# Reordering the first stage of a fused latent-attention and factorised-FFN kernel, with head 1's weights made in unit 0

## The chip, the cores and the metric

One core of a Trainium2 chip runs the kernel; it is launched as one program. The metric is the device time of one execution in microseconds.

## The reference, cut to what matters

```python
xn = layernorm(x)                       # x: 2048 x 512, float32
q = (xn @ wq) per head -> q_nope (128), q_pe (64)     # 16 heads
kva = xn @ wkv_a -> ckv (128), k_pe (64)
ckv = ckv * rsqrt(mean(ckv * ckv) + 1e-6) * kv_norm_scale
k_nope, v = (ckv @ wkv_b) per head
q_pe, k_pe = rope(q_pe), rope(k_pe)
scores = (q_nope @ k_nope.T + q_pe @ k_pe.T) / sqrt(192), causal
attn = softmax(scores) @ v, heads joined, @ wo
ffn = sum over 8 factors of xn @ factors[r], / sqrt(8) + bias
out = x + attn + ffn
```

## The kernel before, in words

The keys are never expanded per head. All heads share 128 normalised latents and 64 turned key elements of each of the 2048 positions; each head's key weights are folded into its query weights (w_abs), its value weights into the output weights (w_vo). Numbers that need float32 precision are kept as pairs of float16 tensors, a high and a low half, and a product is three matmuls (`three`, lines 390 to 392): high by high, high by low, low by high.

**The first stage** (t = 0 to 19, written out by hand on every engine) goes over 16 tiles of 128 rows, two of them a pair p2. SP loads a pair of x (line 1394). VectorE takes mean and variance (`norm_stats`, lines 894 and 898), ScalarE the root (`norm_scale`, 649), VectorE its reciprocal and the shift (904, 906), and ScalarE normalises tile by tile into `xn` (`normalize`, 643), two buffers that overlay `rot`. TensorE transposes (462); ScalarE writes the high half (692), VectorE the low one (1062). `latent_product` on TensorE makes latents and rope keys of a tile. `latent` on ScalarE sums squares (660, 663), `latent` on VectorE takes the reciprocal and turns the keys' first parts (1074 to 1080), `latent_scale` on ScalarE (674) and `turned_keys` on GpSimd (1286) finish them in `kt`, four buffers. `value_parts` on ScalarE copies them to `vH` (681), and that on GpSimd makes `vL` (1278). `keys` transposes them on TensorE (483, 484), with high halves from ScalarE (687, 688) and low ones from VectorE (1087, 1089). Between these stand the weights of heads 0 and 1: the sum over the partitions of squares (`norm`), `scale_pair` on VectorE (921 to 940), transposes of wq and wkv (`wq_transpose`, `kv_transpose`; 1003 to 1028 on VectorE), `w_abs` (1037, 1039) and `w_pe` (732 on ScalarE, 1044 on VectorE). The latent weights `wa` are scaled first by their own norm (`scale_latent`, 835, 1225). At the end stand q_rope(0), q_latent(0) and q_latent(1) on TensorE, the rope parts of the query on ScalarE and GpSimd (763, 1332) and squares of the weights of heads 2 and 3 on ScalarE (695).

**The units** are 64: head by head, for chunks 3, 2, 1, 0 of 512 query rows. A unit has four row blocks r of 128 rows; a row block has chunk + 1 pieces of up to 512 keys (chunk 3, row block 0: 512, 512, 384, 256). `scores` writes one of four banks, `maxima` and `row_max` on VectorE find the maximum of the row over all pieces (1123, 1125, 1135, 1142), `exps` on ScalarE frees the bank (774; it is the first exponential, so the program has a table load ahead of it), `high_parts` (784) and `low_parts` on GpSimd (1341) split the result, and SP issues DMA transposes of it into `pT` (1513). The next unit multiplies them with the values. There are four `ex` buffers, so an exponential waits for the low part four pieces back.

**What sets the order.** Every engine goes through its instructions in the order written; semaphores join them. `fills(i, r)` lists the extra work of unit i behind row block r (weights of later heads, queries of the next unit, outputs), and each engine takes its part of that list in its order. Matmul banks are handed out by `bank_order`. SP's queue is in the order written too: loads of x and of weights (`load_wq` waits for `p_tq` at h - 1 and for the squares of two heads before, `load_wp` for `v_wpe`), then `store_chunk` of the transposed x, then

```python
for m in range(2, 4):
    load_wq(m)
load_wp(2)
store_abs(0)
store_abs(1)
store_pe(0)
```

and then each unit's DMAs. On ScalarE, `squares` (695) waits for the load of its weights: "sqp" for `d_wp`, 64 for each load of a pair of heads.

Of the kernel before, what the change touches and what calls it, by code (L numbers as in the profile page):

```python
# [36 lines left out]

FFN = tuple(QT * c + t for c in ORDER for t in range(QT))
# [10 lines left out]
def chunk(i):  # L49

    return ORDER[i // H]

# [43 lines left out]
def fills(i, r):  # L96

    out = []
    if r == 0:
        if 1 <= i < NU - 1:  # L100
            out.append(("q", i + 1))
        if 1 <= i <= H:
            out.append(("nv", i - 1))
        if i == SQUARED + 1:
            out.append(("nf", 0))
        if i and i % 2 == 0 and i + 2 < H:
            out.append(("nrm", i + 2))
# [11 lines left out]
    if r == 1:  # L119
        if i == 0:  # L120
            out.append(("nrm", 2))
        if i % 2 == 0 and i + 2 < H:
            out.append(("wpe", i + 2))
        if i % 2 == 0 and i + 2 < H:
            out.append(("tq", i + 2))
        if i + 2 <= H + 2:
            out.append(("tkv", i + 2))
# [8 lines left out]
    if r == 2 and i % 2 == 0 and i + 2 < H:  # L136
        out.append(("wpe_low", i + 2))
# [5 lines left out]
    if r == 2:  # L143
        if 1 <= i <= H:
            out.append(("wvo", i - 1))
        if i + 2 < H:
            out.append(("wabs", i + 2))
# [31 lines left out]
def bank_order():  # L179

    pre = []
    for t in range(NT + 4):
        if t < NT:
            pre.append(("xt", t))
        if t == 0:
            pre.append(("na", 0))
        if t == 7:
            pre.append(("nrm", 0))
        if t in (8, 11):
            pre += [("tq", t // 3 - 2), ("tkv", t // 3 - 2)]  # L190
        if t in (10, 13):
            pre.append(("wabs", t // 3 - 3))
        if t % 2 == 1 and 0 <= t // 2 - 2 < NP:
            pre.append(("kT", t // 2 - 2))
        if t == NT + 1:
            pre.append(("pe", 0))
        if t == NT + 2:
            pre.append(("q", 0))
        if t == NT + 3:
            pre.append(("q", 1))  # L200
# [4 lines left out]
def build(nc, x, wq, wkv_a, wkv_b, wo, kvs, factors, bias, rope_t, rope_n, out):  # L205
    ctx = ExitStack()
    with ctx:
# [77 lines left out]
        with nc.sbuf_tensor("early", [P, 2, 4, 2, KE, CH], F16) as region:  # L285
# [8 lines left out]
        xn = rot  # L294
# [11 lines left out]
            "a_sqv", "a_sqo", "a_r4", "a_r8", "a_sqa", "a_sqp", "a_sq0", "a_sq1", "a_sqk", "a_sqf", "a_wa", "a_sd", "a_xn", "a_xt", "a_sq", "a_rms", "a_kk", "a_vH", "a_kT", "a_ff", "a_wpe", "a_wo",  # L306
# [9 lines left out]
            "g_zero", "g_const", "g_sk", "g_sv", "g_fac", "g_bias", "g_rot", "g_parts", "g_pL", "g_kk", "g_vL",  # L316

            "d_wq0", "d_wq1", "d_wo", "d_wp", "d_wk0", "d_wk1", "d_wk2", "d_wk3", "d_wv0", "d_wv1", "d_scl", "d_tab", "d_x0", "d_x1", "d_w", "d_wa", "d_bias",
# [47 lines left out]
        def s_bank(n):  # L366
            return ps[:, n % SBANKS, :]
# [20 lines left out]
        def _(e):  # L388
# [76 lines left out]
            def latent_product(t):  # L465
# [6 lines left out]
                for k4 in range(KE):  # L472
                    ins = three(latent_bank(t // 2)[:, t % 2, :], [x_tile(t, a)[:, k4, :] for a in range(2)],
# [47 lines left out]
            def scores(i, r, p):  # L521
# [83 lines left out]
            for t in range(NT + 4):  # L605
                p = t // 2
                if t < NT:
                    transpose_x(t)
                if t == 0:
                    norm(("na", 0), ("a_sqa",), nra[:, :])  # L610
# [11 lines left out]
                if t == NT + 1:  # L622
                    q_rope(0)
                if t == NT + 2:
                    q_latent(0)
                if t == NT + 3:
                    q_latent(1)
            for i in range(NU + 2):
                for r in range(QT):
                    if i < NU:  # L630
                        for p in range(chunk(i) + 1):
# [6 lines left out]
        def _(e):  # L638
            def normalize(t):
# [3 lines left out]
                e.activation(xn[:, t % 2, :], x_in(t), ACT.Identity, bias=rstd[:, 2, t:t + 1],  # L643
# [34 lines left out]
            def value_parts(p2):  # L678
                ts = slice(2 * p2, 2 * p2 + 2)
                e.wait_ge(z["a_kk"], p2 + 1)  # L680
                e.activation(vH[:, ts, :], kt[p2 % 4][:, :, 0:LORA], ACT.Copy).then_inc(z["a_vH"], 1)

            def keys(p2):
                b = bank(("kT", p2))
                cols = slice(2 * p2 * P, (2 * p2 + 2) * P)
# [4 lines left out]
            def transpose_x(t):  # L690
                e.wait_ge(z["p_xt"], t + 1)
                e.activation(x_tile(t, 0), by4(bank(("xt", t))), ACT.Copy).then_inc(z["a_xt"], 1)
# [130 lines left out]
            normalize(0)  # L823
            norm_scale(1)
            e.wait_ge(z["d_wa"], 16)
            square_sum(wa_f.rearrange("p k n -> p (k n)"), 0, nra[:, :]).then_inc(z["a_sqa"], 1)
            for t in range(NT + 4):
# [3 lines left out]
                if t < NT:  # L831
                    transpose_x(t)
                if t == 0:
                    e.wait_ge(z["v_lat"], 1)
                    e.activation(wa[:, 0, :, :], wa_f, ACT.Identity, bias=eps[:, 2:3], scale=lat[:, 0:1]).then_inc(
                        z["a_wa"], 1)
                if t % 2 == 0 and 0 <= p - 2 < NP:
                    latent_scale(p - 2)
                    value_parts(p - 2)
# [20 lines left out]
            for kind in ("sqk", "sqp", "sq0", "sq1"):  # L860
                squares(kind, 2)
            for i in range(NU + 2):
                for r in range(QT):
# [3 lines left out]
                    for kind, n in fills(i, r):  # L867
                        if soon and kind == "pv":
                            fill(kind, n)
                    for p in range(last + 1):  # L870
# [4 lines left out]
                        if p == 2 and r < 2:  # L875
# [754 lines left out]
```

## Time and profile before

| what | us |
|---|---|
| median of 3 runs | 1525.97 (1525.07 to 1528.10) |
| the profiled execution, its own time | 1529.43 |
| its span | 1527.5 |
| TensorE busy | 1479.1 (97%) |
| VectorE busy | 1012.5 (66%) |
| ScalarE busy | 974.4 (64%) |
| GpSimd busy | 904.7 (59%) |
| mean granted TensorE clock | 0.994 |

The span is that of the profiled execution on its core; 1.9 us lie outside it. Times in the rows below count from its start. PE is TensorE, PEld its weight load, DVE VectorE, ACT ScalarE, POOL GpSimd, and SPq SyncE's queue of DMA issues. "[1.99 <-ACT ex L774]" behind a row says how long the engine was idle before it, and what it waited for.

### The profile page before, as it was taken

The numbers are of one execution on the slowest core, as the hardware profiler recorded it, in microseconds if no ns is written. First come the engines' busy times: TensorE is split into PE (matmuls) and PEld (weight loads), VectorE is DVE, ScalarE is ACT, GpSimd is POOL, SyncE is SP. The second block draws the span as 40 slices with busy tenths as digits, with TensorE's granted clock in tenths as the row PEclk, the third lists the DMA queues.
The fourth block names the chain that finished last, engine by engine and source line by source line (L and its number), as shares of the span: only waits on it lengthen the run. The fifth ranks groups of instructions, "written<-read, shape, count | busy, mean of one in ns | idle before, by whom it ended". The sixth has DMA issues, their size and how long they took to land.

```text
span 1527.5 us, 25754 instructions
## 1 busy us (share of the span) xinstructions
PE 1479.1 (97%) x7908; PEld 758.3 (50%) x7908; DVE 1012.5 (66%) x2563; ACT 974.4 (64%) x2418; POOL 904.7 (59%) x905
## 2 busy tenths in 40 slices
PE   5789999999999999999999999999999999999997
PEld 4444455555544544444445454545545555455553
DVE  6666777767777766655455565656656666676786
ACT  6777676777767476666466667665646666654553
POOL 1367777775655455666465656566645655664552
PEclk9999999999999999999999999999999999999998
DMA  6369989998776588787677677886856677854654
GB/s 219 105 124 206 205 181 189 187 189 163 150 154 139 114 174 168 142 175 138 131 143 139 134 139 146 153 162 134 155 117 138 136 140 149 157 133 98 120 119 99
DMA packets 646598, 227.83 MB, mean 149 GB/s; under 512 B 599360, under 2 KB 612160, under 8 KB 646080
## 3 DMA queue, kind: packets, MB, share of 16 engines
q1 hardware_dynamic: 646464, 226.20, 73.0%
q8 instruction: 65, 1.06, 0.3%
q14 instruction: 69, 0.57, 0.1%
HBM read 65.67 MB, written 17.83 MB: 55 GB/s over the span
## 4 chain that ended last, share of the span: by engine, by line
PE 80%; ACT 7%; DVE 6%; issue 3%; POOL 3%; DMA 1%; SPq 0%; POOLq 0%; ACTq 0%; DVEq 0%
PE ps L390 16%; PE ps L391 16%; PE ps L392 16%; PE ps L534 6%; PE ps L539 6%; PE ps L540 6%; PE ps L536 6%; PE ps L535 6%; ACT ex L774 3%; POOL st L1341 1%; DVE gm L1123 1%; DVE ps L1125 1%; POOL q L1332 1%; DMA st<-x_in 0%; ACT sqr L695 0%
## 5 line engine op out<-in xcount | busy, mean ns | idle before, releaser
L1341 POOL TENSOR_TENSOR st<-ex,st 128x512 f16<-128x512 f32 (+3 forms) x640 | 637.7, 1015 | 504.3 <-ACT st L784 494.5
L774 ACT ACTIVATE ex<-ps,nm,scales 128x512 f32<-128x512 f32 (+3 forms) x640 | 452.5, 709 | 466.8 <-DVE nm L1142 452.8
L1123 DVE TENSOR_REDUCE gm<-ps 128x1 f32<-128x512 f32 (+1 forms) x384 | 249.0, 669 | 176.8 <-PE ps L540 172.6
L784 ACT ACTIVATE st<-ex 128x512 f16<-128x512 f32 (+3 forms) x640 | 341.4, 561 | 5.9
L534 PE MATMUL ps<-kTh,q 128*128 128x512 f16 (+3 forms) x640 | 223.2, 349 | 8.5 <-ACT ex L774 8.4
L539 PE MATMUL ps<-kRh,q 128*128 128x512 f16 (+3 forms) x640 | 222.9, 348 | 4.5 <-POOL q L1332 4.5
L390 PE MATMUL ps<-pT,vH 128*128 128x512 f16 (+3 forms) x640 | 222.4, 347 | 2.4 <-DMA pT<-st 2.4
L536 PE MATMUL ps<-kTh,q 128*128 128x512 f16 (+3 forms) x640 | 223.0, 348 | 0.0
L535 PE MATMUL ps<-kTl,q 128*128 128x512 f16 (+3 forms) x640 | 223.0, 348 | 0.0
L540 PE MATMUL ps<-kRl,q 128*128 128x512 f16 (+3 forms) x640 | 223.0, 348 | 0.0
L391 PE MATMUL ps<-pT,vH 128*128 128x512 f16 (+3 forms) x640 | 222.5, 348 | 0.0
L392 PE MATMUL ps<-pT,vL 128*128 128x512 f16 (+3 forms) x640 | 219.3, 348 | 0.0
L1176 DVE SCALAR_TENSOR_TENSOR acc<-ps,rden,acc 128x512 f32<-128x512 f32 x256 | 189.7, 743 | 4.1 <-PE ps L392 3.7
L1332 POOL TENSOR_TENSOR q<-rot,q 32x512 f16<-32x512 f32 x128 | 149.0, 1164 | 28.6 <-ACT q L763 16.5
L1125 DVE CUSTOM_DVE_ANT_0 ps<-ps,cmask 128x256 f32<-128x256 f32 (+3 forms) x256 | 133.0, 519 | 26.1 <-PE ps L540 23.4
L774 ACT ACTIVATION_READ_ACCUMULATOR ex<-ps,nm,scales 128x1 f32 x640 | 125.7, 196 | 0.0
L1100 DVE SCALAR_TENSOR_TENSOR q<-ps,q 128x512 f16<-128x512 f32 x64 | 44.2, 691 | 114.6 <-ACT q L757 114.6
L390 PE MATMUL ps<-wV,oT 128*128 128x512 f16 x256 | 97.7, 382 | 4.7 <-issue 3.1
L534 PEld LDWEIGHTS ps<-kTh,q 128*128 128x128 f16 x640 | 62.7, 98 | 77.9 <-ACT ex L774 16.8
L391 PE MATMUL ps<-wV,oT 128*128 128x512 f16 x256 | 97.7, 382 | 0.0
L392 PE MATMUL ps<-wV,oT 128*128 128x512 f16 x256 | 97.7, 382 | 0.0
L390 PE MATMUL ps<-xT,wA 128*128 128x512 f16 x256 | 97.0, 379 | 0.0
(200 smaller groups left out, 2145.2 us busy)
## 6 DMA issues: line engine op xcount, KB each, us to landing
wA<-w_abs SPq DMA_DIRECT2D x48, 256.0 KB, 3.0
wV<-w_vo SPq DMA_DIRECT2D x48, 256.0 KB, 3.0
pT<-st SPq DMA_TRANSPOSE x640, 3.3
fland<-factors_in SPq DMA_DIRECT2D x28, 256.0 KB, 3.3
wP<-w_pe SPq DMA_DIRECT2D x24, 256.0 KB, 3.0
wsq<-wq_in SPq DMA_DIRECT2D x16, 256.0 KB, 3.9
wso<-wo_in SPq DMA_DIRECT2D x16, 256.0 KB, 3.1
w_abs<-wA SPq DMA_DIRECT2D x16, 256.0 KB, 2.3
```

The costliest lines, as they stand in the source:

```text
L390: e.matmul(o, a[0], b[0], start=first, stop=False)
L391: e.matmul(o, a[0], b[1], start=False, stop=False)
L392: return e.matmul(o, a[1], b[0], start=False, stop=last)
L534: e.matmul(b, q[:, i % 2, 0, qs], kTh[:, ks], start=True, stop=False)
L535: e.matmul(b, q[:, i % 2, 0, qs], kTl[:, ks], start=False, stop=False)
L536: e.matmul(b, q[:, i % 2, 1, qs], kTh[:, ks], start=False, stop=False)
L539: e.matmul(b, q[:, i % 2, 2, qs], kRh[:, ks], start=False, stop=False)
L540: e.matmul(b, q[:, i % 2, 2, qs], kRl[:, ks], start=False, stop=True).then_inc(z["p_s"], 1)
L774: e.activation(ex[:, n % NEX, 0:keys], s_bank(n)[:, 0:keys], ACT.Exp, bias=nm[:, (i * QT + r) % 4:(i * QT + r) % 4 + 1], scale=scales[:, p ...
L784: e.activation(stage(n, keys)[:, :, 0, :], ex[:, n % NEX, 0:keys].rearrange("p (t n) -> p t n", n=P), ACT.Copy).then_inc(z["a_pH"], 1)
L1123: e.tensor_reduce(m, b, AX_X, ALU.max).then_inc(z["v_max"], 1)
L1341: e.tensor_tensor(s[:, :, 1, :], ex[:, n % NEX, 0:keys].rearrange("p (t n) -> p t n", n=P), s[:, :, 0, :], ALU.subtract).then_inc(z["g_pL" ...
```

## The change

The pairs of tiles are taken in another order: chunk 3's (whose queries come first) and then chunks 0, 1, 2. `PAIRS` maps the pair's place in the order to the pair. The first pair of x is loaded in two DMAs. ScalarE squares the latent weights ahead of the first normalize, and VectorE makes `wa` ahead of the second round. `xn` overlays `ex`. On VectorE, norm_stats goes behind keys in odd t, and norm_scale into even t; on ScalarE latent stands ahead of keys. q_rope(0) and q_latent(0) go to t = 13. `vH` is written by GpSimd. The weights and queries of head 1 are made in unit 0, as fills, as are the squares of head 3's query weights. The first two pieces of unit 0 are scored ahead of the last keys.

```diff
+PAIRS = tuple(QT * c // 2 + n for c in (ORDER[0],) + tuple(range(NC - 1)) for n in range(QT // 2))
...
 def fills(i, r):
     out = []
+    if i == 0:
+        out += [[("tq", 1), ("tkv", 1), ("sq1", 2)], [("wabs", 1), ("nrm", 2), ("wpe", 2)],
+                [("q", 1), ("tq", 2), ("tkv", 2), ("wpe_low", 2)], [("wabs", 2)]][r]
...
-        xn = rot
+        xn = ex
...
         def s_bank(n):
-            return ps[:, n % SBANKS, :]
+            return ps[:, (n + 2) % SBANKS, :]
...
@@ scores @@
-                elif n == 0:
+                if n == 2:
                     e.wait_ge(z["v_kva"], NP)
                     e.wait_ge(z["a_kk"], NP)
-                    e.wait_ge(z["v_kT"], NP)
+                if i == 0 and r == 0 and p < NC - 1:
+                    e.wait_ge(z["v_kT"], (p + 2) * QT // 2)
...
@@ the first stage on TensorE @@
+                if t == 0:
+                    norm(("na", 0), ("a_sqa",), nra[:, :])
                 if t < NT:
                     transpose_x(t)
...
-                if t in (8, 11):
-                    wq_transpose(t // 3 - 2)
-                    kv_transpose(t // 3 - 2)
-                if t in (10, 13):
-                    w_abs(t // 3 - 3)
+                if t == 9:
+                    wq_transpose(0)
+                    kv_transpose(0)
+                if t == 11:
+                    w_abs(0)
...
-                if t == NT + 1:
+                if t == 13:
                     q_rope(0)
+                    q_latent(0)
                 if t == NT + 2:
-                    q_latent(0)
-                if t == NT + 3:
-                    q_latent(1)
+                    scores(0, 0, 0)
+                    scores(0, 0, 1)
...
@@ the first stage on ScalarE @@
             norm_scale(0)
-            normalize(0)
-            norm_scale(1)
             e.wait_ge(z["d_wa"], 16)
             square_sum(wa_f.rearrange("p k n -> p (k n)"), 0, nra[:, :]).then_inc(z["a_sqa"], 1)
+            normalize(0)
...
                 if t % 2 == 0 and 0 <= p - 2 < NP:
                     latent_scale(p - 2)
-                    value_parts(p - 2)
+                if t % 2 == 0 and p + 1 < NP:
+                    norm_scale(p + 1)
...
-                if t == 12:
+                if t == 10:
                     w_pe(0)
-                if t == NT + 3:
+                if t == 14:
                     q_latent(0)
+                if t % 2 == 1 and 0 <= p - 1 < NP:
+                    latent(p - 1)
+                if t == NT:
+                    rope_parts(0)
                 if t % 2 == 1 and 0 <= p - 2 < NP:
                     keys(p - 2)
-                if t % 2 == 1 and 0 <= p - 1 < NP:
-                    latent(p - 1)
-                if t % 2 == 1 and p + 2 < NP:
-                    norm_scale(p + 2)
-            q_latent(1)
-            rope_parts(0)
-            for kind in ("sqk", "sqp", "sq0", "sq1"):
+            for kind in ("sqk", "sqp", "sq0"):
                 squares(kind, 2)
...
@@ the first stage on VectorE @@
             norm_stats(0)
             norm_scale(0)
+            scale_latent()
             norm_stats(1)
-            norm_scale(1)
+            e.wait_ge(z["a_wa"], 1)
+            e.scalar_tensor_tensor(out=wa[:, 1, :, :], in0=wa_f, scalar=lat[:, 0:1], in1=wa[:, 0, :, :],
+                                   op0=ALU.mult, op1=ALU.subtract).then_inc(z["v_wa"], 1)
...
-                if t == 7:
+                if t == 8:
                     scale_pair(0)
-                if t in (8, 11):
-                    wq_transpose(t // 3 - 2)
-                    kv_transpose(t // 3 - 2)
-                if t in (10, 13):
-                    w_abs(t // 3 - 3)
-                if t == 13:
+                if t == 10:
+                    wq_transpose(0)
+                    kv_transpose(0)
+                if t == 12:
+                    w_abs(0)
                     w_pe(0)
-                if t == NT + 2:
+                if t == 14:
                     q_rope(0)
-                if t == NT + 3:
                     q_latent(0)
+                if t == NT + 1:
+                    latent(NP - 1)
+                if t % 2 == 0 and p + 1 < NP:
+                    norm_scale(p + 1)
                 if t % 2 == 1 and 0 <= p - 2 < NP:
                     keys(p - 2)
-                if p + 2 < NP:
-                    if t % 2 == 0:
-                        norm_stats(p + 2)
-                    else:
-                        norm_scale(p + 2)
-            q_latent(1)
+                if t % 2 == 1 and p + 2 < NP:
+                    norm_stats(p + 2)
...
@@ units on VectorE @@
+                    if (i, r) == (0, 3):
+                        q_latent(1)
...
@@ GpSimd @@
-                e.wait_ge(z["a_vH"], p2 + 1)
+                e.wait_ge(z["a_kk"], p2 + 1)
+                e.tensor_copy(vH[:, ts, :], values).then_inc(z["g_vH"], 1)
...
             for p2 in range(NP):
                 turned_keys(p2)
-                value_parts(p2)
-            q_rope(0)
-            rope_parts(0)
+                if p2 == NP - 2:
+                    rope_parts(0)
+                if p2 < NP - 2:
+                    value_parts(p2)
...
@@ SP @@
-                e.wait_ge(z["v_xt"], QT * (c + 1))
+                e.wait_ge(z["v_xt"], QT * (c + 2))
...
                 load_wq(m)
             load_wp(2)
             store_abs(0)
-            store_abs(1)
             store_pe(0)
...
+                    if (i, r) == (0, 2):
+                        store_abs(1)
```

## Rows read from the trace of the kernel before

**Rows 1.** Busy time and matmul clock by stretch: us, PE, PEld, DVE, ACT, POOL, PEclk, DMA
```profile
0.00:96.00 96.00, 63.22 (x441) 44.90 (x441) 60.98 (x191) 66.74 (x179) 27.72 (x51) 0.95 0.46 140
82.80:86.20 3.40, 3.40 (x10) 1.27 (x9) 1.39 (x2) 2.74 (x8) 1.75 (x2) 0.51 0.00 0
96.00:1527.50 1431.50, 1415.91 (x7467) 713.43 (x7467) 951.51 (x2373) 907.69 (x2241) 876.97 (x855) 1.00 0.75 150
```

**Rows 2.** Timeline of ScalarE, first stage: start, us, engine, line, operation, tiles
```profile
...
9.39 0.83 ACT L695 ACTIVATE sqr<-vH 128x768 bf16<-128x768 f32 x1
...
25.29 0.80 ACT L643 ACTIVATE rot<-st,rstd 128x512 f32<-128x512 f32 x1
...
26.47 0.62 ACT L695 ACTIVATE sqr<-wsq 128x512 bf16<-128x512 f32 x1
...
27.70 0.36 ACT L687 ACTIVATE kTh<-ps 128x256 f16<-128x256 f32 x1
...
29.23 0.28 ACT L649 ACTIVATE rstd<-mv,eps 128x2 f32<-128x2 f32 x1
...
42.99 0.81 ACT L674 ACTIVATE kt<-ps,eps,ssq 128x128 f32<-128x128 f32 x2 [0.54 <-DVE ktmp L1080]
...
52.38 0.80 ACT L643 ACTIVATE rot<-acc,rstd 128x512 f32<-128x512 f32 x1
...
73.44 0.61 ACT L695 ACTIVATE sqr<-wsp 128x512 bf16<-128x512 f32 x1
...
75.39 1.28 ACT L774 ACT_TABLE_LOAD   x1
...
80.96 0.78 ACT L774 ACTIVATE ex<-ps,nm,scales 128x512 f32<-128x512 f32 x1 [4.29 <-DVE nm L1142]
...
```

**Rows 3.** Timeline of VectorE, first stage
```profile
...
33.66 0.15 DVE L921 TENSOR_REDUCE tot<-ps 128x1 f32<-128x3 f32 x1
...
35.24 0.41 DVE L1087 SCALAR_TENSOR_TENSOR kTl<-ps,kTh 128x256 f16<-128x256 f32 x1
...
36.16 0.16 DVE L1074 RECIPROCAL ssq<-ssq 128x2 f32<-128x2 f32 x1
...
36.69 0.68 DVE L1062 TENSOR_TENSOR early<-ps,early 128x512 f16<-128x512 f32 x1
37.29 0.74 DVE L1003 TENSOR_SCALAR wX<-ps,scales 128x512 f16<-128x512 f32 x1
...
39.38 1.28 DVE L894 BATCH_NORM_STATS2 stats<-acc 128x6 f32<-128x512 f32 x2
...
40.85 0.66 DVE L1062 TENSOR_TENSOR early<-ps,early 128x512 f16<-128x512 f32 x1
...
54.30 0.68 DVE L1037 TENSOR_SCALAR wA<-ps 128x512 f16<-128x512 f32 x1
...
55.62 0.74 DVE L1044 SCALAR_TENSOR_TENSOR wP<-wsp,scales,wP 128x512 f16<-128x512 f32 x1
...
66.01 0.69 DVE L1110 TENSOR_TENSOR rot<-ps,tab 128x512 f32<-128x512 f32 x1 [0.37 <-PE ps L392]
...
```

**Rows 4.** Timeline of TensorE, end of the first stage and unit 0
```profile
...
63.15 0.38 PE L390 MATMUL ps<-xT,wP 128*128 128x512 f16 x1
...
68.33 0.27 PE L483 MATMUL ps<-ident,kt 128*128 128x128 f32 x1
...
81.88 0.39 PE L534 MATMUL ps<-kTh,q 128*128 128x512 f16 x1 [1.99 <-ACT ex L774]
...
96.06 0.39 PE L534 MATMUL ps<-kTh,q 128*128 128x512 f16 x1 [1.60 <-ACT ex L774]
...
```

**Rows 5.** Timeline of GpSimd, ahead of the first scores
```profile
...
72.75 2.37 POOL L1332 TENSOR_TENSOR q<-rot,q 32x512 f16<-32x512 f32 x2 [3.29 <-ACT q L763]
...
```

**Rows 6.** Timeline of SP's queue, the four loads of wp for heads 2 and 3
```profile
...
56.39 2.02 SPq L1428 DMA_DIRECT2D wsp<-wq_in  x4
...
```

**Rows 7.** The same four loads by tile: from issue to landing
```profile
DMA to landing us min/median/max: 1.9/2.5/2.9
```

More of the change, by code:

```diff
@@ L51, in chunk, with tile, both @@
     return ORDER[i // H]
+def tile(n):
+    return 2 * PAIRS[n // 2] + n % 2
+def both(p):
+    return slice(2 * PAIRS[p], 2 * PAIRS[p] + 2)
 def pieces(c, r):
@@ L119, in fills @@
     if r == 1:
[L120 to L126, printed above, removed]
+        if i and i % 2 == 0 and i + 2 < H:
+            out += [("wpe", i + 2), ("tq", i + 2)]
+        if i and i + 2 <= H + 2:
             out.append(("tkv", i + 2))
@@ L145, in fills @@
             out.append(("wvo", i - 1))
-        if i + 2 < H:
+        if i and i + 2 < H:
             out.append(("wabs", i + 2))
@@ L472, in latent_product @@
                 for k4 in range(KE):
-                    ins = three(latent_bank(t // 2)[:, t % 2, :], [x_tile(t, a)[:, k4, :] for a in range(2)],
+                    ins = three(latent_bank(t // 2)[:, t % 2, :], [x_tile(tile(t), a)[:, k4, :] for a in range(2)],
                                 [wa[:, a, k4, :] for a in range(2)], k4 == 0, k4 == KE - 1)
@@ L630, in _ @@
                     if i < NU:
-                        for p in range(chunk(i) + 1):
+                        for p in range(2 if i == 0 and r == 0 else 0, chunk(i) + 1):
                             scores(i, r, p)
@@ L642, in normalize @@
                     e.wait_ge(z["p_xt"], t - 1)
-                e.activation(xn[:, t % 2, :], x_in(t), ACT.Identity, bias=rstd[:, 2, t:t + 1],
+                e.activation(xn[:, t % 2, :], x_in(tile(t)), ACT.Identity, bias=rstd[:, 2, t:t + 1],
                              scale=rstd[:, 1, t:t + 1]).then_inc(z["a_xn"], 1)
@@ L676, in latent_scale @@
                 ins.then_inc(z["a_kk"], 1)
[L678 to L681, printed above, removed]
             def keys(p2):
                 b = bank(("kT", p2))
-                cols = slice(2 * p2 * P, (2 * p2 + 2) * P)
+                cols = slice(2 * PAIRS[p2] * P, (2 * PAIRS[p2] + 2) * P)
                 e.wait_ge(z["p_kT"], p2 + 1)
@@ L691, in transpose_x @@
                 e.wait_ge(z["p_xt"], t + 1)
-                e.activation(x_tile(t, 0), by4(bank(("xt", t))), ACT.Copy).then_inc(z["a_xt"], 1)
+                e.activation(x_tile(tile(t), 0), by4(bank(("xt", t))), ACT.Copy).then_inc(z["a_xt"], 1)
             def square_sum(w, at, total):
@@ L869, in _ @@
                             fill(kind, n)
+                    early = ("q", "wo", "parts", "sqv") + (("sq1",) if i == 0 else ())
                     for p in range(last + 1):
@@ L874, in _ @@
                             high_parts(i, r, p - 1)
-                        if p == 2 and r < 2:
+                        if p == (2 if i else 3) and (r < 2 or i == 0):
                             for kind, n in fills(i, r):
-                                if kind in ("q", "wo", "parts", "sqv"):
+                                if kind in early:
                                     fill(kind, n)
@@ L884, in _ @@
                             continue
-                        if last < 2 or r >= 2 or kind not in ("q", "wo", "parts", "sqv"):
+                        if last < 2 or (r >= 2 and i) or kind not in early:
                             fill(kind, n)
@@ L1067, in latent @@
                 ts = slice(2 * p2, 2 * p2 + 2)
-                cos = ropen[:, ts, 0, :].unsqueeze(2).broadcast_to([P, 2, 2, HALF])
+                rows = both(p2)
+                cos = ropen[:, rows, 0, :].unsqueeze(2).broadcast_to([P, 2, 2, HALF])
                 halves = b[:, :, LORA:QH].rearrange("p t (a n) -> p t a n", a=2)
@@ L1078, in latent @@
                 for a in range(2):
-                    ins = e.tensor_tensor(ktmp[:, p2 % 4, :, a, :], halves[:, :, 1 - a, :], ropen[:, ts, 1 + a, :], ALU.mult)
+                    ins = e.tensor_tensor(ktmp[:, p2 % 4, :, a, :], halves[:, :, 1 - a, :], ropen[:, rows, 1 + a, :], ALU.mult)
                 ins.then_inc(z["v_kva"], 1)
@@ L1356, in _ @@
             scale_keys(0)
-            scale_keys(2)
-            scale_values(3)
             for p2 in range(NP):
                 turned_keys(p2)
-                value_parts(p2)
-            q_rope(0)
-            rope_parts(0)
+                if p2 == NP - 2:
+                    rope_parts(0)
+                if p2 < NP - 2:
+                    value_parts(p2)
+                if p2 == 1:
+                    scale_keys(2)
+                if p2 == 2:
+                    scale_values(3)
+                if p2 == NP - 3:
+                    q_rope(0)
+            value_parts(NP - 2)
+            value_parts(NP - 1)
             for i in range(NU + 1):
```

72 lines of the change are left out of this document (35 added, 37 removed).

## The prediction

> **What bounds the kernel now.** The page's first part has TensorE busy for 97% of the span, and busy time by stretch shows where the rest lies: it is idle 32.8 us of the first 96 us and 15.6 of the 1431.5 behind them [rows 1]. What it has to do after that point is the same in both kernels but for a little that the change moves across it. So the change is worth what it does to the time at which TensorE becomes full, and I read the first 96 us engine by engine, in order of time: ScalarE [rows 2], VectorE [rows 3], TensorE [rows 4]. The figures to follow are the start of normalize for tiles 6 and 14 (25.29 and 52.38), the first exponential's release of TensorE (row block 1's scores start at 81.88) and row block 3's start. I write N(t) for normalize of tile t, X for its transposes on TensorE, H and D for the high and low halves (ScalarE, VectorE), and a round for two tiles.
>
> **The front gains some 3 us.** The square of the latent weights ran at 9.39 [rows 2], behind the second pair's norm_scale. Now it follows norm_scale(0), at about 6.05, some 3.3 earlier. From there I place the new order with the rows' durations: N(2) at 11.9, N(4) at 16.3, N(6) at 22.5 against 25.29, so 2.8 early. Loading the first pair in two parts is costed at nothing: both parts are awaited before the pair's mean. One more issue on SP (0.45) delays later loads, which are wanted more than 1 us after they land.
>
> **The rounds get longer.** This is the step on which I differ from a count of work. Removed per round is the ScalarE copy to vH (0.32); head 1's weights leave, 2.09 + 1.32 of VectorE; w_pe and the queries come in. But norm_stats now stands on VectorE behind keys of an odd t, keys wait for ScalarE's keys, which stands behind latent, H and N; and norm_scale, which the next N needs, stands behind norm_stats. That closes a ring through both engines. Its hops: N and H 1.18 (25.29 to 26.47), ScalarE's keys and latent 1.53 (27.70 to 29.23, there in the other order) [rows 2] and 0.14 until VectorE's keys begin; VectorE's keys and the two instructions of norm_scale 0.92, statistics 1.47 [rows 3]; latent on VectorE to latent_scale on ScalarE 0.65, that itself 0.75, norm_scale's root 0.31, hand-overs 0.15. The sum is 7.1 us a round. Where VectorE has extra work E in the even half, the branch by latent_scale and the root (1.71) is replaced by latent to D 0.53, D 0.60 and E, thus 6.5 + E. E is scale_pair 1.58 at t = 8, the transposes' halves 2.09 at t = 10, w_abs 1.32 with w_pe 0.66 at t = 12 [rows 3]. Rounds from N(6): 7.1 with the two squares 1.23 [rows 2] 8.3; then 8.1, 8.6 and 8.5, together 33.5. Before, the same four took 52.38 - 25.29 = 27.1. So N(14) starts at 56.0, 3.6 later than before, and the front's gain is gone.
>
> **The tail is shorter, up to the last scores.** The queries' 24 matmuls took 63.15 to 68.33, 5.2 us [rows 4], ahead of the last keys; now they start when w_pe is done (55.6) and end at 60.8. They are not free there, since X(14) is queued behind them and H, D behind that: D(14) starts at 61.9. Then on VectorE D 0.6, q_rope 2.1, q_latent 0.6, D(15) 0.6, keys 0.66, latent 0.6: 67.1. ScalarE's latent_scale and rope_parts: 68.4. GpSimd's rope_parts 2.4 [rows 5]: 70.9. There the first scores, held since 69, go on; keys(7) is queued behind them on TensorE: transposes end at 72.9, VectorE's keys at 74.3, and scores of pieces 2 and 3 (640 columns, five matmuls a column, 1.35) at 75.7. GpSimd's new tensor_copy (128x256) has no row; between nothing and the 0.67 of its two-input neighbour I take 0.4, and either end is hidden, because value_parts of the last pairs stands behind turned_keys(7). To 75.7 I add 1.3 for the clock: after an idle time of 1.99 us (row of 81.88) [rows 4] the old TensorE ran 3.4 us at a granted clock of 0.51 [rows 1], the level of 1.2 GHz, twice the time a matmul; the new tail has idle stretches of 1.9 and 1.4. Bounds: 0 and 1.7. So the last score ends at 77.0 against 79.9.
>
> **The new wait, on SP.** load_wq(3) waits until head 1's transposes have left wsq (p_tq at 2). These are now a fill of row block 0, behind all its scores: 77.5. load_wp(2) is queued behind load_wq(3) on SP, and ScalarE computes squares("sqp", 2) of that load before its first exponential. That order is not changed. Four loads of wp take 2.02 to issue, the fourth starting 1.5 after the first [rows 6], and land 2.5 later (1.9 to 2.9) [rows 7]; with 0.45 for load_wq(3): 77.5 + 4.5 = 82.0. Then sqp and sq0, 1.34 [rows 2]; the table load, 1.28 [rows 2], which lay hidden before, since ScalarE then idled 4.29 us up to 80.96; the first exponential and its release 0.9: row block 1's scores start at 85.5 against 81.88 [rows 4], 3.6 later. Without this wait they would start at 79.0.
>
> Where the table load stands decides 1.3 of it. In the rows it comes behind the squares of the same loop. The Trainium skill (ScalarE activation tables: per-element evaluation and per-set limits, Table sets in the compiler and the runtime) says that the back end places these loads per block by the longest run. By a run that took in the squares, the load would stand ahead of the awaited one, hidden, and the sum would be +3.8 in place of +5.1. The trace shows it behind them, and I go by the trace.
>
> **Unit 0 gives back 1.5.** TensorE gets 3.8 there: q(1) 2.6, w_abs(1) 0.67, transposes 0.55 (from the 0.2155 a 512 columns of those matmuls). The transposes lie in the wait ahead of row block 1 and w_abs(1) in that ahead of row block 2. Behind block 2 stand q(1) and tq(2), 3.2, where w_abs(2) and 1.6 of idle time were [rows 4]; 0.8 sticks out, and w_abs(2), 0.67, comes behind block 3. VectorE ends block 3's maxima 1 to 2 later, within the time of pe(2) on TensorE. SP's load_wq(4) now waits for tq(2) ahead of the block's DMA transposes, 5 us before these are wanted. Bounds: 0.5 to 3.
>
> **Sum:** 3.6 + 1.5 = +5.1 us. The profiled execution took 1529.4 (span 1527.5), 3.5 above the median of 1525.97; the sum is a difference and is put on the median: 1531.1. A measurement here tells some 0.2%, 3 us.
>
> **The rivals.**
> - The ring stays open, as the rounds before did not wait so (faster). Place: the four rounds from N(6). Bound by busy time, VectorE has 22.7 us there and ScalarE 21.5. At 24 the sum is 5.1 - 9.5 = -4.4, 1521.6. For it: both engines were nearly always busy from 30 to 50. Against: the orders show each hop. It decides below 25.4.
> - The rounds keep their 27.1: -1.3, 1524.7. Then the shorter tail and the new wait cancel.
> - The loads do not hold ScalarE: 79.0 in place of 85.5, so -1.4, 1524.6. For it only that the queue might be entered earlier than I read; the condition on p_tq speaks against.
> - The overlap in the first stage fails in more places: 2 us more in the rounds, the clock low for all of blocks 0 and 1, 3 in unit 0: about +9, 1535. 8 us of idle TensorE ahead of block 1 speak for it.
> - Scoring the first two pieces early does not do what it says: their last matmuls wait for GpSimd's rope parts until 70.9 and hold keys(7) up. That is in my sum; where GpSimd is quicker by 1, so is the last score.
>
> **How the numbers follow.** Forecast (+2.5 to +7.5) 0.49; open ring 0.13; old rounds 0.16; no hold 0.08; more stalls 0.14. Faster is the open ring and the low edge of two others, 0.17; the same 0.23; slower 0.60. Terms of unknown size: rounds 2 either way, clock -1.3 and +0.4, landing 0.6, unit 0 -1 and +1.5. The range takes the cases near -2.5 in and ends at +9: 1523.5 to 1535.0.
>
> **What would show it.** N(6) near 22.5 and N(14) near 56; VectorE idle at odd t ahead of keys with ScalarE as releaser. q_rope's matmuls near 55.6. ScalarE waiting for wsp's load with TensorE idle some 8 us, then sqp, sq0, the table load and the exponential in a row. Row block 1's scores at 85.5, block 3 to unit 1 1.5 longer. N(14) below 49 would prove the ring wrong; an exponential that waits for VectorE's nm, and not for the load, the SP step. Gaps of TensorE behind unit 1 that were not there before would make the whole frame wrong.

## The result, and the profile of the changed kernel

The changed kernel takes 1542.78 us (median of 4 runs, 1542.05 to 1543.55) against 1527.03 us of the kernel before on the same chip (1525.07 to 1529.99): a ratio of 1.0102, 95% interval 1.0083 to 1.0120, or 15.75 us slower. The forecast was slower by 5.1 us and its range ended at +9. The direction was right; the time lies outside the range.

The profiled execution took 1543.55 us with a span of 1541.7 us, 14.2 above the span of before. The windows, with the columns of [rows 1]:

```profile
0.00:96.00 96.00, 56.51 (x367) 42.37 (x368) 49.62 (x157) 56.01 (x152) 23.12 (x52) 0.85 0.40 126
47.76:52.70 4.94, 4.94 (x32) 4.78 (x33) 1.48 (x5) 1.86 (x6) 0.00 (x0) 0.50 0.26 103
59.25:66.28 7.03, 7.03 (x26) 2.98 (x27) 2.09 (x8) 3.46 (x10) 0.87 (x2) 0.76 0.00 0
92.42:97.50 5.08, 5.08 (x13) 1.85 (x14) 1.29 (x2) 4.26 (x12) 1.98 (x2) 0.52 0.00 0
96.00:1541.70 1445.70, 1427.13 (x7543) 720.56 (x7540) 964.16 (x2406) 915.04 (x2259) 885.24 (x862) 1.00 0.75 149
```

The second to the fourth of them are TensorE's work behind a wait in the fourth round, the queries, and row block 1's scores. The busy times of its engines, from the page:

```profile
PE 1483.6 (96%) x7908; PEld 762.9 (49%) x7908; DVE 1013.8 (66%) x2563; ACT 971.1 (63%) x2410; POOL 908.4 (59%) x913
```

They are those of before within 5 us: the work is the same, its place is not. In the first 96 us TensorE is now busy for 56.5 us, where it had 63.2 [rows 1], and at a mean clock of 0.85. The loss is complete when unit 1's first scores start: 103.16 before, 117.94 after, 14.8 us later. From there to the end it is 1424.3 us before and 1423.8 after, so the frame of the prediction, that only the start counts, holds.

These are the times at which it can be followed (us from the start of the span; N(t) is normalize of tile t):

| point | before | after | predicted |
|---|---|---|---|
| N(6) | 25.29 | 23.74 | 22.5 |
| N(14) | 52.38 | 59.41 | 56.0 |
| the queries of unit 0, first matmul to the next work | 63.15 to 68.33 | 59.25 to 66.11 | 55.6 to 60.8 |
| end of the first scores and transposes of head 1 | | 84.1 | 77.5 |
| wp of heads 2 and 3 has landed | | 88.85 | 82.0 |
| row block 1's scores start | 81.88 | 92.42 | 85.5 |
| unit 1's first scores start | 103.16 | 117.94 | 108.3 |

The last predicted figure is 103.16 + 3.6 + 1.5. What ScalarE does at these points, from its timeline:

```profile
7.23 0.84 ACT L701 ACTIVATE sqr<-vH 128x768 bf16<-128x768 f32 x1 [1.77 <-DMA vH<-wkv_a_in]
...
23.74 0.81 ACT L654 ACTIVATE ex<-st,rstd 128x512 f32<-128x512 f32 x1 [0.43 <-DVE rstd L913]
...
52.11 0.28 ACT L671 ACTIVATE junk<-ps 128x128 bf16<-128x128 f32 x1 [2.16 <-PE ps L401]
...
59.41 0.81 ACT L654 ACTIVATE ex<-acc,rstd 128x512 f32<-128x512 f32 x1 [1.88 <-DVE rstd L913]
...
66.75 0.60 ACT L698 ACTIVATE early<-ps 128x512 f16<-128x512 f32 x1 [3.81 <-PE ps L471]
...
88.85 0.63 ACT L701 ACTIVATE sqr<-wsp 128x512 bf16<-128x512 f32 x1 [6.83 <-DMA wsp<-wq_in]
...
90.20 1.28 ACT L780 ACT_TABLE_LOAD   x1
...
91.49 0.78 ACT L780 ACTIVATE ex<-ps,nm,scales 128x512 f32<-128x512 f32 x1
```

The wait for wsp is there, and the two squares, the table load and the exponential follow it in a row. The chain of work that ended last goes through the same place (start, length, what):

```profile
83.61 0.45 PE ps L423 x4
84.08 0.38 SPq L1423
84.51 0.61 SPq L1450
85.17 0.50 SPq L1450
85.71 0.51 SPq L1450
86.26 2.57 DMA wsp<-wq_in
88.89 0.49 issue
89.38 0.80 ACT sqr L701 x3
90.20 1.28 ACT L780
```

The transposes of head 1 (L423) release load_wq(3) on SP (L1423), the four loads of wp (L1450) come behind it, and ScalarE's squares wait for the last of them. TensorE's own rows:

```profile
47.76 1.11 PE L471 MATMUL ps<-ident,ex 128*128 128x128 f32 x4 [3.71 <-DVE wX L1012]
...
92.42 0.61 PE L545 MATMUL ps<-kTh,q 128*128 128x512 f16 x1 [8.26 <-ACT ex L780]
...
114.67 0.23 PE L399 MATMUL ps<-wKV,wX 128*128 128x128 f16 x1 [2.17 <-DVE q L1108]
...
117.94 0.38 PE L545 MATMUL ps<-kTh,q 128*128 128x512 f16 x1
```

The second row is the one that [rows 4] has at 81.88 with 1.99 us of idle time. The first and the third are waits that the prediction does not have. On VectorE the ring shows as predicted, keys of an odd t waiting for ScalarE's keys:

```profile
34.86 0.43 DVE L1095 SCALAR_TENSOR_TENSOR kTl<-ps,kTh 128x256 f16<-128x256 f32 x1 [0.84 <-ACT kRh L694]
...
53.78 0.42 DVE L1095 SCALAR_TENSOR_TENSOR kTl<-ps,kTh 128x256 f16<-128x256 f32 x1 [3.11 <-ACT kRh L694]
```

### The profile page after: what moved, and what is told of

It reads as the page before. It is cut to its first block, busy times and chain, and to the rows that moved or that the text cites. A ratio compares the mean times of both kernels' runs of the same rounds, so it can differ in the third digit from the quotient of the medians.

```text
span 1541.7 us, 25755 instructions
## 1 busy us (share of the span) xinstructions
PE 1483.6 (96%) x7908; PEld 762.9 (49%) x7908; DVE 1013.8 (66%) x2563; ACT 971.1 (63%) x2410; POOL 908.4 (59%) x913
## 4 chain that ended last, share of the span: by engine, by line
PE 81%; DVE 7%; ACT 7%; issue 4%; DMA 1%; POOL 0%; SPq 0%; ACTq 0%; POOLq 0%; DVEq 0%
PE ps L399 16%; PE ps L400 16%; PE ps L401 16%; PE ps L545 7%; PE ps L550 6%; PE ps L551 6%; PE ps L546 6%; PE ps L547 6%; ACT ex L780 3%; DVE gm L1131 1%; DVE ps L1133 1%; DVE stats L901 0%; ACT sqr L701 0%; ACT wV L747 0%; DVE q L1108 0%
```

## The experiments

Each kernel is the changed one with the edit shown, but for the last, which starts from the kernel before. Ratios are to the kernel before, with their 95% intervals; the changed kernel's is 1.0102 [1.0083, 1.0120]. Spans are those of the profiled executions, one for each kernel, so a difference of spans holds scatter: the four kernels here that have the same order up to N(14) reach it at 58.65 to 59.41. "By the medians" is the same difference from the median times.

**The loads of wp ahead of the load that waits.** SP's queue alone is changed.

```diff
-            for m in range(2, 4):
-                load_wq(m)
+            load_wq(2)
             load_wp(2)
+            load_wq(3)
```

> The changed kernel with one line moved on SP: load_wp(2) ahead of load_wq(3). My theory (ScalarE's squares of wp hold the first exponential, as the load stands behind load_wq(3), which waits for head 1's transposes in row block 0): wp lands near 77, the squares follow sqk without a wait, the first exponential starts at 84.6 to 85 in place of 91.49, row block 1's scores at 85.5 to 86 in place of 92.42, and the kernel is 6.5 to 7.5 us faster than the changed one. Rival (the exponential would have waited for VectorE's maximum and GpSimd anyway, the load only seems to be last): under 2 us.

Measured: 1531.30 us, ratio 1.0025 [1.0016, 1.0034]; the span is 1530.1, 11.6 shorter than the changed kernel's (11.5 by the medians, where 6.5 to 7.5 was expected). SP's queue and ScalarE:

```profile
71.22 4.01 SPq L1450 DMA_DIRECT2D wsp<-wq_in  x4
...
80.57 0.61 ACT L701 ACTIVATE sqr<-wsp 128x512 bf16<-128x512 f32 x1
...
81.18 0.61 ACT L701 ACTIVATE sqr<-wsq 128x512 bf16<-128x512 f32 x1
...
81.90 1.28 ACT L780 ACT_TABLE_LOAD   x1
...
83.31 0.78 ACT L780 ACTIVATE ex<-ps,nm,scales 128x512 f32<-128x512 f32 x1
...
89.31 0.78 ACT L780 ACTIVATE ex<-ps,nm,scales 128x512 f32<-128x512 f32 x1 [0.80 <-DVE nm L1150]
```

The squares no longer wait. The first exponential starts 8.2 us earlier (83.31 for 91.49), of which 0.8 was there already at N(14), 58.65 for 59.41, ahead of the place of the edit. The hold is thus worth some 7.4; 0.3 of it is that the queries took 6.6 us in this execution and 6.9 in the changed kernel's. Row block 1's first exponential then comes 6.0 us behind row block 0's, and in the changed kernel 8.4 (91.49 to 99.90): another 2.4, which the expectation had left out, and this is the clock. Window from the start of row block 1's scores:

```profile
84.24:88.20 3.96, 3.96 (x24) 2.14 (x24) 2.99 (x6) 3.96 (x12) 0.85 (x1) 1.00 0.53 188
```

The granted clock is 1.00, the level of 2.4 GHz, behind an idle time of 1.44 us; in the changed kernel it was 0.52, the level of 1.2 GHz, for 5.1 us behind 8.26 us of idle time. Unit 1's first scores start 10.6 us earlier (107.34); the remaining 1.0 of the 11.6 lies behind them. So the hold with its slow clock is one of the two largest causes, and dearer than the 6.5 that the prediction gave it.

**The queries of unit 1 earlier on VectorE.** TensorE waited 2.17 us at 114.67 for VectorE's q_latent(1), because w_abs(2) gets the bank that q(1) had been in, and VectorE read it behind row block 3's maximum.

```diff
-                    if (i, r) == (0, 3):
-                        q_latent(1)
...
                             fill(kind, n)
+                    if (i, r) == (0, 2):
+                        q_latent(1)
```

> The changed kernel with VectorE's q_latent(1) put behind its fills of row block 2, ahead of the maxima of row block 3. Theory (the matmul bank of w_abs(2) is the one that q(1) was made in, and VectorE reads it only behind row block 3's maximum; TensorE waited 2.17 us): TensorE's wait ahead of w_abs(2) goes, row block 3's maximum comes 0.6 later, the kernel is 1.5 to 2.2 us faster than the changed one. Rival (TensorE would then wait the same time for the exponentials of row block 3 at unit 1's first scores): 0 to 0.5.

Measured: 1538.52 us, ratio 1.0072 [1.0059, 1.0084]; span 1536.7, 5.0 shorter (4.3 by the medians, more than the 1.5 to 2.2 expected). TensorE:

```profile
111.27 0.22 PE L399 MATMUL ps<-wKV,wX 128*128 128x128 f16 x1
...
114.53 0.38 PE L545 MATMUL ps<-kTh,q 128*128 128x512 f16 x1
```

w_abs(2) follows the scores at once and unit 1 starts 3.4 us earlier. The wait was real and its cause this bank. Of the 3.4, 0.9 was there already when row block 1's scores started (91.53 for 92.42), ahead of the place of the edit, and 0.2 came in row block 1. From row block 2's scores to unit 1's it is 2.3 us less (99.76 to 114.53, before the edit 100.82 to 117.94), which is the edit's worth. The rest of the 5.0 lies behind unit 1's start, and its cause was not found.

**Banks of their own for head 0's weights.** In the round of t = 12 ScalarE's latent waited 2.16 us for TensorE, and TensorE 3.71 us for VectorE's wX (47.76). The idea was that the bank turn made that wait.

```diff
+        own = {("tq", 0): 2, ("tkv", 0): 3, ("wabs", 0): 2}
+        turns = [k for k in pre_uses if k not in own]
```

> The changed kernel with the first stage's tq(0), tkv(0) and w_abs(0) in the two banks that hold no latents and no scores yet, in place of the four that transposes and keys take in turn. Theory (TensorE's X(11) waited 3.71 us for VectorE to read tq(0), and keys(4) 2.3 us for w_abs(0), because they get the same bank): both waits go, the rounds from N(12) to N(14) take 8.5 to 8.7 in place of 10.76, and the kernel is 2 to 2.7 us faster. Rival (the rounds are bound by VectorE's own work there, the bank wait hides in it): under 0.7.

Measured: 1542.23 us, ratio 1.0095 [1.0081, 1.0109]; span 1541.0. No gain that can be told, where 2 to 2.7 us was expected. TensorE:

```profile
48.66 0.27 PE L402 MATMUL ps<-wKV,wX 128*128 128x128 f16 x1 [3.66 <-DVE wKV L1038]
```

The same wait, 3.66, has moved from the transposes of x to w_abs(0) itself, which needs the halves that VectorE is still making. So the bank alone is not the cause: with it out of the way, TensorE's order holds the latents as long.

**The same banks, and w_abs(0) behind the latents and keys of t = 11.**

```diff
-                if t == 11:
-                    w_abs(0)
                 if 0 <= t - 2 < NT:
...
                     keys(p - 2)
+                if t == 11:
+                    w_abs(0)
```

> The changed kernel with own banks as in the run e3 and TensorE's w_abs(0) behind latent_product(9) and keys(3) of t = 11. The run e3 showed that the bank was not what held TensorE: with banks of its own it waited as long for the halves of w_abs(0) itself. Theory (w_abs(0) stands ahead of latent_product(9), so ScalarE's latent(4) starts 2.2 us late): N(12) to N(14) falls from 10.6 to 8.5, 1.5 to 2.3 us faster than the changed kernel. Rival (the time is lost on VectorE in that round, not by the latents): under 0.5.

Measured: 1539.75 us, ratio 1.0083 [1.0069, 1.0097]; span 1537.1, 4.6 shorter (3.0 by the medians; 1.5 to 2.3 was expected). ScalarE:

```profile
48.61 0.81 ACT L657 ACTIVATE ex<-acc,rstd 128x512 f32<-128x512 f32 x1 [1.26 <-DVE rstd L916]
...
49.81 0.27 ACT L674 ACTIVATE junk<-ps 128x128 bf16<-128x128 f32 x1
...
57.11 0.81 ACT L657 ACTIVATE ex<-acc,rstd 128x512 f32<-128x512 f32 x1 [1.88 <-DVE rstd L916]
```

latent no longer waits, and the round from N(12) to N(14) takes 8.50 us in place of 10.76, which is the 8.5 of the prediction. This edit lifts both holds, the bank and the order; w_abs(0) late with the old banks was not run, so how much each would bring alone is open. TensorE's clock changed with it too. Its window from w_abs(0) to the end of the latents of tile 9:

```profile
48.45:51.02 2.57, 2.28 (x28) 2.07 (x28) 0.82 (x2) 2.34 (x8) 0.00 (x0) 1.00 0.00 0
```

w_abs(0) and the 12 matmuls of the latents behind it took 0.67 and 0.99 us there, and 1.28 and 1.92 in the changed kernel, at 0.50 behind the wait of 3.71. So some 1.5 of the 2.16 us that latent had waited is slow clock behind TensorE's wait. The queries, which start 2.3 us earlier, ran at 1.00 and ended 4.0 earlier: that is the part of the 4.6 beyond the round.

**The statistics of x in their old place.** norm_stats back to even t and norm_scale back to odd t; this is the part that the prediction holds for the ring.

```diff
-                if t % 2 == 0 and p + 1 < NP:
-                    norm_scale(p + 1)
+                if t == 0:
+                    norm_scale(1)
...
-                if t % 2 == 1 and p + 2 < NP:
-                    norm_stats(p + 2)
+                if p + 2 < NP:
+                    if t % 2 == 0:
+                        norm_stats(p + 2)
+                    else:
+                        norm_scale(p + 2)
```

> The changed kernel with norm_stats and norm_scale of pairs 2 to 7 where they stood before (VectorE: statistics in even t, scale in odd t; ScalarE: the root at the end of odd t). Theory (statistics behind keys and the scale behind both close a ring of 7.1 us a round): N(6) to N(14) falls from 35.7 to 28 to 31, and the kernel is 4 to 7 us faster than the changed one. Rival (the rounds are long because of the extra weights' work and the bank waits, whatever the place of the statistics): under 1.5.

Measured: 1531.03 us, ratio 1.0025 [1.0014, 1.0036]; span 1530.1, 11.6 shorter (11.8 by the medians; 4 to 7 was expected). ScalarE and TensorE:

```profile
22.14 0.81 ACT L654 ACTIVATE ex<-st,rstd 128x512 f32<-128x512 f32 x1
...
48.16 0.81 ACT L654 ACTIVATE ex<-acc,rstd 128x512 f32<-128x512 f32 x1
```
```profile
102.36 0.29 PE L399 MATMUL ps<-wKV,wX 128*128 128x128 f16 x1 [2.15 <-DVE q L1110]
```

The four rounds take 26.0 us (22.14 to 48.16), against 35.7 in the changed kernel and 27.1 before, and less than the 28 to 31 expected. In the round of t = 12 TensorE now waits 1.97 us for VectorE's wX in place of 3.71 and runs at 1.00 behind it. The place of the statistics, with what it did in the round of t = 12, cost 9.7 us, and the rest of the new order is itself a little faster than the old one. The hold of wp is still in this kernel: row block 1 waits 8.23 us.

**Both of the large ones: old place of the statistics, and wp first.**

```diff
-            for m in range(2, 4):
-                load_wq(m)
+            load_wq(2)
             load_wp(2)
+            load_wq(3)
...
@@ and norm_stats, norm_scale as in the experiment above @@
```

> The changed kernel with the loads' order of e1 and the statistics' places of e4. Theory (two separate losses, and the slow clock of row block 1 goes with the wait): row block 1's scores near 72.5, the first two row blocks 6 us apart, 19 to 22 us faster than the changed kernel, 4 to 7 faster than the one before. Rival (both take time from the same wait, so that the second brings little once the first is gone): 12 to 15 faster than the changed one.

Measured: 1521.82 us, ratio 0.9968 [0.9956, 0.9981]; span 1519.1, 22.6 shorter than the changed kernel's, where the two alone gave 11.6 each. By the medians it is 21.0 against 11.5 and 11.8. They add up within the intervals: they are separate causes. This version is already faster than the kernel before, by 0.3%.

**All five edits together.**

```diff
@@ wp first; q_latent(1) at (0, 2); banks of their own; @@
@@ statistics in their old place; w_abs(0) behind keys @@
```

> The changed kernel with all the mends: loads' order, statistics' places, q_latent(1) early on VectorE, own banks, w_abs(0) behind the latents on TensorE. Theory (each loss is its own): 2 to 5 us faster than e7, 7 to 11 faster than the kernel before, row block 1's scores near 71. Rival (TensorE's queries at t = 13, which hold X(14) up, then set the end of the stage and take the rest back): no more than 1 us faster than e7.

Measured: 1517.26 us, ratio 0.9935 [0.9922, 0.9948]; span 1514.6, 4.5 shorter than the one before it. N(14) starts at 47.34, row block 1's scores at 72.33, unit 1's first scores at 93.10. ScalarE still waits in the tail:

```profile
55.17 0.60 ACT L701 ACTIVATE early<-ps 128x512 f16<-128x512 f32 x1 [4.30 <-PE ps L474]
```

The transposes of tile 14 stand behind the 24 matmuls of the queries.

**Those five, and the queries at t = 15.** They now lie behind the transposes of tile 15 and not ahead of those of tile 14. The list that hands out the banks moves with them, and their halves on VectorE as those on ScalarE.

```diff
-                if t == 13:
+                if t == 15:
                     q_rope(0)
...
-                if t == 14:
+                if t == 16:
                     q_latent(0)
...
                 if p2 == NP - 2:
+                    q_rope(0)
                     rope_parts(0)
...
-                if p2 == NP - 3:
-                    q_rope(0)
```

> e5 with the queries at t = 15, behind the last transposes of x, their halves on VectorE behind latent(6). Theory (the queries at t = 13 keep both copy engines waiting 4 us for X(14), which a later place would spare, against latent products 14 and 15 and the last keys being queued behind them): N(14) unchanged, row block 1's scores 0 to 2 us earlier than in e5. Rival (midway is right, the last latents pay the whole 5.2 us): 2 to 4 us slower than e5.

Measured: 1513.14 us, ratio 0.9909 [0.9895, 0.9922]; span 1511.0, the shortest of all, 3.6 below the one before it; 0 to 2 was expected. TensorE:

```profile
61.47 0.39 PE L553 MATMUL ps<-kRh,q 128*128 128x512 f16 x1 [1.07 <-POOL q L1349]
...
68.72 0.39 PE L548 MATMUL ps<-kTh,q 128*128 128x512 f16 x1 [1.44 <-ACT ex L783]
```

Row block 1's scores start at 68.72, 13.2 us before those of the kernel before [rows 4], and unit 1's first scores at 89.49 against 103.16. Of the 3.6, 1.0 was there at N(14) already (46.30 for 47.34), where the two kernels have the same order; from N(14) to row block 1's scores it is 2.6 less (22.4 for 25.0), and this is the edit's worth.

**The late queries alone**, with all the rest as changed: the parts of the diff above, on the changed kernel, and nothing else.

> The changed kernel with only the queries put later, as in e8 (t = 15 on TensorE, behind the last transposes of x; halves on VectorE in t = 16). Theory (the place midway costs some 4 us, as e8 against e5 shows, whatever else the kernel does): 3 to 5 us faster than the changed kernel, ScalarE's wait of 3.8 for X(14) gone. Rival (in the changed kernel the loads' wait on SP hides it, since all is late there): under 1.5, with a first exponential that waits for wsp as before.

Measured: 1538.45 us, ratio 1.0072 [1.0060, 1.0084]; span 1536.0, 5.7 shorter (4.3 by the medians). ScalarE:

```profile
85.20 0.63 ACT L701 ACTIVATE sqr<-wsp 128x512 bf16<-128x512 f32 x1 [6.65 <-DMA wsp<-wq_in]
```

From N(14) to row block 1's scores it is 3.1 us less (29.9 for 33.0), and 1.7 of that is the clock: the queries now took 5.2 us at 1.00. The rest of the 5.7 is a better clock in row block 1 (7.5 us between the first exponentials of blocks 0 and 1, for 8.4) and scatter ahead of N(14) and behind unit 1's start. The wait for wsp stays as long, since the load is issued behind the same scores: a gain ahead of it is passed on, the hold is paid again.

**The front alone**, on the kernel before: the latent weights' squares (the diff), and likewise their norm on TensorE ahead of the first transposes and scale_latent on VectorE ahead of norm_stats(1); nothing else of the change.

```diff
             norm_scale(0)
-            normalize(0)
-            norm_scale(1)
             e.wait_ge(z["d_wa"], 16)
             square_sum(wa_f.rearrange("p k n -> p (k n)"), 0, nra[:, :]).then_inc(z["a_sqa"], 1)
+            normalize(0)
+            norm_scale(1)
```

> The kernel before with one part of the change alone: the latent weights' norm first (ScalarE squares them ahead of the first normalize, TensorE sums ahead of the first transposes, VectorE scales ahead of the second statistics). Theory (this part of the change is sound and gives 1.5 to 2.5 us at N(6), and TensorE is full only from unit 0 on, so a good half of it arrives): 1 to 2.5 us faster than the kernel before. Rival (VectorE and ScalarE are nearly always busy from 25 to 50 us and take it back): within 0.7 of the kernel before.

Measured: 1527.15 us, ratio 0.9995 [0.9986, 1.0003]: no difference that can be told. N(6) starts at 24.24, 1.05 earlier than before [rows 2], and N(14) at 52.27, 0.11 earlier. The gain is gone within one round: N(8) starts at 31.65, where before has it at 31.75. What takes it is a load. GpSimd scales head weights (wsk) ahead of turned_keys(0), and waits for their DMA; TensorE's keys(0) wait 2.44 us for turned_keys(0), and ScalarE's keys 0.85 for these:

```profile
24.99 0.61 POOL L1306 TENSOR_TENSOR wsk<-wsk,scl 128x256 f32<-128x256 f32 x1 [13.49 <-DMA wsk<-wkv_b_in]
...
26.93 0.30 PE L483 MATMUL ps<-ident,kt 128*128 128x128 f32 x1 [2.44 <-POOL kt L1285]
...
27.59 0.38 ACT L687 ACTIVATE kTh<-ps 128x256 f16<-128x256 f32 x1 [0.85 <-PE ps L484]
```

Before, the same load let GpSimd start at 24.06, and ScalarE's keys did not wait: a load that did not come earlier with the rest holds the front. The span is 1524.1, 3.4 below that of before, but not for this. Row block 1 ran at a granted clock of 1.00 there (81.67 to 86.00) in the profiled execution, where before has 0.51 [rows 1] behind the same idle time of 1.99 us, which is 1.7 us, and 1.5 of the 3.4 lies behind unit 1's first scores.

## Why the prediction was wrong in its size

**What bounds the kernel: right.** The whole loss lies ahead of unit 1, and the rest of the kernel took 0.6 us less.

**The front: right in kind, too large.** The squares of the latent weights were put at 6.05. They started at 7.23, behind 1.77 us of waiting for their load (the first row of ScalarE above). The step left out that wait: once the work stood early enough, the DMA became its bound. N(6) came at 23.74, 1.2 later than 22.5. How late the load is differs by execution: in the other kernels with this front on the changed one ScalarE waited 0.80 to 1.98 us for it.

**The ring: right in its sums, but for the fourth round.** The first three rounds from N(6) took 8.26, 8.07 and 8.58 us, where the sum had 8.3, 8.1 and 8.6. The fourth took 10.76 for 8.5. The step that failed is "w_abs 1.32 with w_pe 0.66 at t = 12" as all that the weights cost in that round: they were counted on VectorE alone. TensorE waited 3.71 us for VectorE's halves: in the changed kernel at the transposes of tile 11, which get the bank that VectorE still reads, and with banks of their own at w_abs(0) itself. The latents of tile 9 are queued behind, and they and w_abs(0) then ran at 0.50, which is some 1.5 of the 2.16 us that ScalarE's latent waited. With both holds lifted the round took 8.50. The rival of the open ring, and that of the old rounds, fell with these rows, and moving the statistics back showed the ring from the other side, with rounds of 6.4, 6.0, 6.5 and 7.2 us, 26.0 in place of 35.7.

**The queries: "at 55.6, end at 60.8" had the place right and the duration wrong.** They took 6.9 us (59.25 to the next work at 66.11) and not 5.2, at a granted clock of 0.76. The prediction allowed for a clock loss of up to 1.7, but behind the new tail's idle stretches and not here. The end of the first transposes came at 84.1, 6.6 late: 3.65 of it was there when the queries began, 1.7 came from their clock, and 1.2 behind them. That the transposes of tile 14 stand behind the queries was in the prediction (D(14) at 61.9), but no other place was weighed: a later one is worth 2.6 us where the other faults are mended, and 3.1 in the changed kernel, 1.7 of that being the clock.

**The new wait on SP: right in every link, nearly in size.** From the end of the transposes to the landing it took 4.8 us (84.06 to 88.85) against 4.5; from the landing to row block 1's scores 3.6 (88.85 to 92.42) against 3.5. The table load stood behind the squares, on the path, as the prediction took from the rows and not from the rule of the Trainium skill (ScalarE activation tables: per-element evaluation and per-set limits, Table sets in the compiler and the runtime) read as placing it ahead; the row at 90.20 with 1.28 us decides it for this kernel. The rival without a hold fell.

**Unit 0: 1.5 longer by the prediction, 4.2 in fact.** From row block 1's scores to unit 1's took 21.3 us before and 25.5 after. The sum named work alone, and two stalls came on top of it: row block 1 at the low clock, 0.7 longer than before (8.41 between the first exponentials of blocks 0 and 1, 7.68 before), and VectorE's late read of q(1), which held the bank of w_abs(2) for 2.17. Without the two, 1.3 is left, near the 1.5 predicted. The term priced what TensorE executes there and when VectorE ends, but not who reads a bank last.

**In sum:** 14.8 us at unit 1 against 5.1. Of the 9.7 missing, 6.9 are there at row block 1's scores: 3.65 when the queries start (the front 1.2, the fourth round 2.3, the rest rounding), 1.7 from their clock, 1.2 from waits and clock behind them, 0.3 from the loads. The other 2.8 are unit 0's two stalls (2.9). Slow clock where the prediction had none is an estimated 3.9 of it: 1.5 in the fourth round, 1.7 in the queries, 0.7 in row block 1. The rival of more stalls, +9 with a chance of 0.14, had the right picture (longer rounds, slow clock, 3 in unit 0) and was still too small, and the range ended at it, with nothing left above.

## What to carry to other kernels

An order written by hand for several engines is priced by its loops through two engines, not by the busy time of either: here one placement of 1.5 us of statistics, with what followed from it, cost 9.7 us. For each operation that is moved, ask three things of each engine that it touches: what is queued behind it while it waits (SP's loads and TensorE's products here), who reads last the bank that it gets, and from which point a load and no longer the order bounds it. And ask it of the loads that do not move: in the run of the front alone one of them took the gain. Stalls of TensorE came out dearer than their length where the granted clock fell behind them.

## What the runs showed of the hardware that had not been expected

- The granted clock behind short idle times is not the same from one execution to the next. Row block 1's scores ran at 0.50 to 0.52 behind 1.99 us (before), 8.23 and 8.26 us of idle time, and at 1.00 behind 1.44 us (four kernels), but also behind 1.99 us in the run of the front alone. It moves row block 1 by 1.7 us (7.68 to 5.99 between the first exponentials of blocks 0 and 1) to 2.4 us.
- The queries, dense work of 24 matmuls, ran at 0.76 (59.25 to 66.28). TensorE had waited 2.28 us for VectorE up to 58.48, and from 59.99 to 62.98 its matmuls stand 0.43 us apart, twice the 0.22 of the others. With the statistics in their old place they ran at 1.00, at t = 15 too, and at t = 13 with w_abs(0) late, where the waits ahead of them were 1.39 and 1.03 us.
- Idle time of that length does not decide it alone. In unit 0 a wait of 2.15 us ahead of w_abs(2) (statistics in their old place) was followed by 3.6 us at 0.54; the wait of 2.17 us at the same place in the changed kernel was followed by none, nor were those of 2.15 and 2.16 us in five other kernels. The windows of the one and of the other:

```profile
102.36:106.00 3.64, 3.64 (x19) 2.15 (x20) 1.38 (x2) 3.64 (x12) 3.08 (x4) 0.54 1.03 196
```
```profile
112.00:118.00 6.00, 3.83 (x28) 1.93 (x27) 3.92 (x9) 3.95 (x11) 5.61 (x6) 1.00 0.78 163
```

What else goes into it is open. It is worth up to 2.4 us a time, and executions of one kernel differ by such amounts: ten of the kernel before, on one chip, ran from 1524.75 us at a mean clock of 0.999 to 1529.59 at 0.994.
- GpSimd's tensor_copy of 128x256 from float32 to float16, for which before had no row, took 0.40 us in every pair, the value estimated:

```profile
57.41 0.40 POOL L1285 CAST vH<-kt 128x256 f16<-128x256 f32 x1
```
